# Writing out the four rounds of an attention loop, without the look-ahead of the last one

## The reference, cut to what matters

```python
scores = jnp.einsum('bhqd,bhkd->bhqk', q, k) / jnp.sqrt(jnp.asarray(hd, x.dtype))
causal = jnp.tril(jnp.ones((T, T), bool))
scores = jnp.where(causal, scores, jnp.asarray(-jnp.inf, x.dtype))
attn = jax.nn.softmax(scores, axis=-1)
y = jnp.einsum('bhqk,bhkd->bhqd', attn, v)
```

## Time and profile before

| | |
|---|---|
| median of 3 runs | 2978.18 us (2977.76 to 2980.15) |
| profiled execution, its own time | 2973.09 us |
| its span in the profile | 2971.4 us |
| `attention`, TensorE from the head part's first matmul to the last sum | 839.9 to 2042.0 us |
| the four rounds, on TensorE | 891.2 to 2038.1 us |
| granted TensorE clock, mean over the span | 0.916 |

### The profile page before, as it was taken

One profiled execution on the slowest core, in us unless ns is written; L12 is line 12 of the kernel. 1 busy time (PEld: TensorE's weight loads), 2 busy tenths in 40 slices (PEclk: granted clock), 3 DMA queues, 4 the chain that ended last, 5 costly groups with the idle time before them and its releaser, 6 DMA issues. The chain is left out here.

```text
span 2971.4 us, 45370 instructions
## 1 busy us (share of the span) xinstructions
PE 2544.9 (86%) x13518; PEld 1649.7 (56%) x13519; DVE 1460.8 (49%) x3131; ACT 911.1 (31%) x1734; POOL 1442.0 (49%) x951
## 2 busy tenths in 40 slices
PE   6799999897769999999999999994999239999970
PEld 4677667775534444444444444442777138878860
DVE  4545454012587776777677767774344221111115
ACT  3511001112405555555555556553011010000000
POOL 4443244023236675667566757674233355466413
PEclk9999999998959999999999999997999669999985
DMA  7365655456454241425151515243565474455339
GB/s 259 98 171 169 191 171 185 173 212 205 147 112 102 58 119 42 111 51 126 34 126 39 122 37 126 55 116 114 174 190 166 156 271 163 141 168 171 113 114 394
DMA packets 227095, 422.70 MB, mean 142 GB/s; under 512 B 31596, under 2 KB 82508, under 8 KB 226772
## 3 DMA queue, kind: packets, MB, share of 16 engines
q1 hardware_dynamic: 186116, 283.90, 34.2%
q0 software_dynamic: 25344, 92.29, 8.6%
q10 hardware_dynamic: 15440, 44.09, 3.9%
HBM read 265.72 MB, written 145.53 MB: 138 GB/s over the span
## 5 line engine op out<-in xcount | busy, mean ns | idle before, releaser
L1307 POOL TENSOR_TENSOR t_two<-t_prob 128x1024 f32<-128x1024 f32 (+1 forms) x321 | 686.7, 2161 | 176.1 <-ACT t_prob L1186 111.6
L1186 ACT ACTIVATE t_prob<-t_scores_psum 128x512 f32<-128x512 f32 (+3 forms) x1280 | 618.3, 538 | 471.3 <-PE t_scores_psum L1080 260.2
L1053 PE MATMUL t_seen_psum<-t_k_stack,t_q_stack 97*128 97x512 f32 (+2 forms) x1356 | 561.0, 425 | 49.6 <-DVE t_q_stack L1202 22.6
L1214 DVE TENSOR_REDUCE t_part<-t_seen_psum 128x1 f32<-128x512 f32 x812 | 508.5, 683 | 179.1 <-PE t_seen_psum L1053 170.0
L1076 PE MATMUL t_scores_psum<-t_q_stack,t_k_stack 98*128 98x512 f32 (+3 forms) x1280 | 513.7, 409 | 9.6 <-issue 6.6
L1076 PEld LDWEIGHTS t_scores_psum<-t_q_stack,t_k_stack 98*128 98x128 f32 x1280 | 249.0, 195 | 313.3 <-ACT t_prob L1186 159.9
L1053 PEld LDWEIGHTS t_seen_psum<-t_k_stack,t_q_stack 97*128 97x128 f32 x1356 | 277.9, 205 | 99.2 <-DVE t_part L1214 41.3
L1220 DVE CUSTOM_DVE_ANT_0 t_seen_psum<-t_seen_psum,t_causal 128x128 f32<-128x128 f32 (+3 forms) x544 | 264.4, 505 | 117.1 <-PE t_seen_psum L1053 106.8
L1094 PE MATMUL t_y_acc_psum<-t_prob,t_v 128*32 128x512 f32 (+3 forms) x2576 | 306.2, 548 | 0.0
L670 PE MATMUL e_acc_psum<-e_w_hi,e_x_hi 128*128 128x512 f32 x576 | 231.1, 401 | 0.0
L671 PE MATMUL e_acc_psum<-e_w_lo,e_x_hi 128*128 128x512 f32 x576 | 226.6, 393 | 0.0
(11 more groups left out here) (227 smaller groups left out, 3699.6 us busy)
## 6 DMA issues: line engine op xcount, KB each, us to landing
e_w_raw<-in_expert_w POOLq DMA_DIRECT2D x64, 512.0 KB, 4.4
scratch_rows<-f_y POOLq DMA_DIRECT2D x48, 512.0 KB, 15.1
e_x<-scratch_rows SPq DMA_DIRECT2D x38, 512.0 KB, 4.1
t_q_stack<-scratch_q_hi SPq DMA_DIRECT2D x72, 256.0 KB, 4.8
t_k_stack<-scratch_k_hi SPq DMA_DIRECT2D x72, 256.0 KB, 5.0
scratch_rows<-e_y ACTq DMA_DIRECT2D x36, 512.0 KB, 4.7
f_w_raw<-in_wmod SPq DMA_DIRECT2D x8, 2048.0 KB, 10.8
f_w_raw<-in_w_attn SPq DMA_DIRECT2D x24, 512.0 KB, 7.5
```

Of the source, the lines that this page charges most:

```text
L1053: nc.tensor.matmul(seen[:, n % BANKS, 0:width], q_stack[par][0:SEEN, h, t0:t0 + P], k_stack[par][0:SEEN, h, c * CH:c * CH + width], start= ...
L1186: nc.scalar.activation(prob[:, step % RING, h, c0:CH], scores[:, score_bank(step, h), c0:CH], ACT.Exp, scale=1.0 / math.sqrt(D)).then_inc( ...
L1214: nc.vector.tensor_reduce(dst, seen[:, n % BANKS], AX.X, ALU.max).then_inc(seen_free, 1)
L1307: nc.gpsimd.tensor_tensor(two[:, pair % 2, heads, c0:CH], a, b, ALU.add).then_inc(two_ready, 1)
```

## The change

The four rounds are written out on all five engines: `for i in range(G // 2)` is a Python loop, and i is a number. With that the values that are waited for are constants. A new test, `due(i, n)`, drops the entries of `order` behind the last one of an existing group in the last round: 73 `see` and 2 `turn`, on TensorE, VectorE and SyncE. The loads of steps 40 to 79 of the last round are dropped as well (24 of 256 KB for q and k, 4 of 256 KB for v). The closing waits of SyncE count what is left.

```diff
--- before.py
+++ after.py
@@ -889,7 +889,7 @@
 
         def ended(i, step, lag):
 
-            return [wi for wi in range(-1, 0 if isinstance(i, int) else W) if last_step(wi) == step - lag]
+            return [wi for wi in range(-1, 0 if i == G // 2 else W) if last_step(wi) == step - lag]
 
         def first_column(step):
 
@@ -928,6 +928,11 @@
         HEAD = until(AHEAD)
         entries_of = lambda step: range(until(AHEAD + PACE * step), until(AHEAD + PACE * (step + 1)))
         assert STEPS % RING == 0
+        LAST_OWN = max(n for n, entry in enumerate(order) if entry[1] < 2)
+
+        def due(i, n):
+
+            return i < G // 2 - 1 or n <= LAST_OWN
 
         def share(step, slot):
 
@@ -1016,7 +1021,7 @@
 
                 half, at = divmod(step, STEPS // 2)
                 c, part = divmod(at - Y_LAG, len(PARTS) + 1)
-                if not 0 <= c < NQ:
+                if not 0 <= c < NQ or (half == 1 and i == G // 2 - 1):
                     return
                 par, g = (1, ds(i * 2 + 1)) if half == 0 else (0, ds((i * 2 + 2) % G))
                 if (c, part) == (0, 0):
@@ -1027,21 +1032,21 @@
                     sp.dma_start(v[par][:, c * TPC:(c + 1) * TPC, :],
                                  v_d[g, :, c * TPC:(c + 1) * TPC, :].rearrange("g p k n -> (g p) k n")).then_inc(loaded[par][c], 16)
 
-            with sp.Fori(0, G // 2) as i:
+            for i in range(G // 2):
                 for step in range(STEPS):
                     finish(i, step)
                     fetch(i, step)
                     for n in entries_of(step):
-                        if order[n][0] == "turn":
+                        if order[n][0] == "turn" and due(i, n):
                             sp.wait_ge(minus_ready, i * W + unit_of(order[n]) + 1)
                             load_row(sp, order[n][1] % 2, order[n][2], unit_of(order[n]) % 2)
             for step in range(STORE_LAG + 1):
                 finish(G // 2, step)
             sp.wait_ge(stored, 32 * (G * NQ + 3))
             for c in range(NQ):
-                sp.wait_ge(loaded[0][c], LOADS * (G // 2))
+                sp.wait_ge(loaded[0][c], LOADS * (G // 2 - 1))
             for b in range(2):
-                sp.wait_ge(row_loaded[b], ROW * (G * NQ // 2 + 1 + sum(e[0] == "turn" and unit_of(e) % 2 == b for e in order[:HEAD])))
+                sp.wait_ge(row_loaded[b], ROW * (G * NQ // 2 + 1))
 
         @block.tensor
         def _(pe):
@@ -1086,7 +1091,7 @@
                 wi, kt = steps[step]
                 par, qc = UNITS[wi]
                 c0 = first_column(step)
-                if step >= 0 or isinstance(i, int):
+                if step >= 0 or i > 0:
                     pe.wait_ge(exp_done, (i * STEPS + step) * HG + HG + BANKS)
                 if kt == 0:
                     pe.wait_ge(y_free, i * W + wi + 1)
@@ -1133,11 +1138,13 @@
 
                 for n in share(step, slot):
                     what, dg, qc, c, h, j = order[n]
-                    if what == "see" and dg > 0 and (c, h, j) == (0, 0, 0):
+                    if not due(i, n):
+                        continue
+                    if what == "see" and dg > 0 and (c, h, j) == (0, 0, 0) and (dg < 2 or i < G // 2 - 1):
                         pe.wait_ge(loaded[dg % 2][qc], i * LOADS + LOADS)
                     advance(i, n)
 
-            with pe.Fori(0, G // 2) as i:
+            for i in range(G // 2):
                 for step in range(STEPS):
                     wi = steps[step][0]
                     if steps[step][1] == 0:
@@ -1175,7 +1182,7 @@
                 for wi in ended(i, step, TOTAL_LAG):
                     take_total(i, wi)
 
-            with act.Fori(0, G // 2) as i:
+            for i in range(G // 2):
                 for step in range(STEPS):
                     c0 = first_column(step)
                     act.wait_ge(y_done, i * STEPS + step + 1)
@@ -1269,11 +1276,12 @@
                 for wi in ended(i, step, INV_LAG):
                     invert(i, wi)
 
-            with dve.Fori(0, G // 2) as i:
+            for i in range(G // 2):
                 for step in range(STEPS):
                     for slot in range(HG):
                         for n in share(step, slot):
-                            advance(i, n)
+                            if due(i, n):
+                                advance(i, n)
                         if slot == 1:
                             finish(i, step)
             for step in range(DIVIDE_LAG + 1):
@@ -1320,7 +1328,7 @@
                 for wi in ended(i, step, SPLIT_LAG):
                     split(i, wi)
 
-            with pool.Fori(0, G // 2) as i:
+            for i in range(G // 2):
                 for step in range(STEPS):
                     finish(i, step)
                     if step % 2 == 1:
```

## The result

| | before | after |
|---|---|---|
| median | 2977.97 us (2971.82 to 2980.15, 4 runs) | 2924.17 us (2923.66 to 2929.28, 4 runs) |
| the profiled execution, its own time | 2973.09 us | 2924.26 us |
| its span | 2971.4 us | 2922.4 us |

The ratio is 0.9825, with a 95% interval from 0.9808 to 0.9842. The medians are 53.8 us apart, the two profiled executions 48.8.

A forecast was written before the change was run, and what follows sets the result against it. TensorE was taken to set the pace of the rounds. Turns 30 plus last round 9 made 39 us off the profiled 2973.1, so 2934; with the median 5.1 higher, 2939 us, range 2928 to 2956.

The forecast's parts named there:

- What costs nothing: Register instructions beside busy TensorE, other engines' jumps under its stop, and dropped loads: priced at zero.
- the two terms: The priced gains: 30 us at the three turns between rounds and 9 us in the last round.
- what bounds the kernel: In the rounds of `attention`, TensorE sets the pace, busy 63.34 of the last 63.9 us.
- The turns: Three passages between rounds: 4.2 us of gaps and some 6 of lower clock each, 30 us together.
- the clock falls anyway: Rival at the rounds' first steps: gaps go, clock still drops; gain 22 us, median 2956; 1 in 10.
- the turns stay: Rival at the turns: the stop is not the jump's and remains; 9 us left, 2969; 4 in 100.
- The last round: Last 19 steps of the last round: dropping 73 `see` and two `turn` gives 9 us, lower bound 4.
- The step of 2.62: Last round: a step without row sums takes 2.62 us, where it was 2.85.
- the pair of 6.10: Last round: two steps with 512 columns, without `see`, take 6.10 us, a gain of 0.45 a step.
- Late blocks of code: Rival in the rounds: straight code's 16 KB blocks come late, TensorE stops 2.25 us each; slower; 3 in 100.
- The offset of 5.1 us: Median of the runs before stood 5.1 us above the profiled execution; added to 2934 to give 2939.

The follow-up runs named there:

- tensore_alone_in_the_loop: Against the kernel before: all engines written out except TensorE, which keeps the hardware loop; last round's look-ahead kept. 2972.82 us, ratio 1.0005.
- idle_put_back: Changed kernel, with TensorE made to wait at each turn for two small DMAs one after the other. 2949.59 us, ratio 0.9909 to the kernel before.
- written_out_only: Against the kernel before: rounds written out on all engines, all work and loads of the last round kept. 2931.74 us, ratio 0.9855.
- changed_again: The changed kernel itself, run again on another chip against the kernel before. 2925.68 us, ratio 0.9831.
- idle_put_back_once: Changed kernel, with TensorE made to wait at each turn for one small DMA. 2930.79 us, ratio 0.9845 to the kernel before.
- changed_all_later: Changed kernel with VectorE's addition, GpSimd's split, SyncE's load of a_y and its stores one step later. 2937.63 us, ratio 0.9881 to the kernel before.
- changed_later_addition: Changed kernel with VectorE's addition of a_y and GpSimd's split one step later. 2945.83 us, ratio 0.9893 to the kernel before.

## Why the prediction missed, point by point

- **The step that failed is "What costs nothing"**, the term that was put at zero. In its place the profiles show 8.4 us outside the two terms, and the runs 8 to 10: writing out alone gained 39 and 41, where the turns are 31. The two terms that had a price were right, and so was what bounds the kernel.
- **What bounds the kernel**, TensorE, was right: with all other engines changed and TensorE left in its loop, nothing is gained.
- **The turns**: 30 us forecast, 31.1 in the profiles. The reading by marks held, and so did both halves of it: the jump is needed for the stop (`tensore_alone_in_the_loop`), and a stop without a jump is enough for the lower clock (`idle_put_back`). No "issue" gap is left, and the clock is 1.00 in the first steps, so the rivals "the clock falls anyway" and "the turns stay" are out. The Trainium skill, Advanced Engine Details and Errata, Control Flow Timing, gives about 108 ns for a compare-and-branch, which would have made 0.3 us of the term. The trace does not agree: with the loop on TensorE alone the three taken branches took 3327 to 3777 ns, and their removal brought the whole term. (In the kernel before they took 3303, 3908 and 3421 ns; the 3362 that I gave as the lower end is a median over four, with the branch that isn't taken.)
- **The last round**: 9 us forecast, 9.4 in the profiles and 9.8 against `written_out_only`. The step of 2.62 and the pair of 6.10 were nearly met. Timeline of all engines, one pair of the last round and the wait at its end:

```profile
1962.92 0.96 PE L1081 MATMUL t_scores_psum<-t_q_stack,t_k_stack 98*128 98x512 f32 x3
...
1963.54 2.07 ACT L1193 ACTIVATE t_prob<-t_scores_psum 128x512 f32<-128x512 f32 x4 [1.48 <-PE t_scores_psum L1081]
...
1964.19 0.50 PE L1081 MATMUL t_scores_psum<-t_q_stack,t_k_stack 98*128 98x512 f32 x1 [0.30 <-ACT t_prob L1193]
...
1965.62 0.96 PE L1081 MATMUL t_scores_psum<-t_q_stack,t_k_stack 98*128 98x512 f32 x3
...
1969.15 0.98 PE L1081 MATMUL t_scores_psum<-t_q_stack,t_k_stack 98*128 98x512 f32 x3
...
1990.29 0.64 PE L1112 MATMUL t_total_psum<-t_two,t_ones 128*32 128x256 f32 x8 [1.85 <-POOL t_two L1315]
```

  Head 3's score comes 1.27 us after the first (1.21 forecast) and waits for ScalarE, 0.30 us; a pair takes 1969.15 - 1962.92 = 6.23 us, and its first step 2.70. The last row sums wait 1.85 us for GpSimd, as before. The clock did not fall, though TensorE has more idle time.
- **Late blocks of code** did not come: no "issue" gap stands between the rounds, with q8 at 54 blocks in the 1087 us of the rounds, one in 20 us instead of the 17 forecast. I had overlooked that the written-out code is shorter: q8 brings TensorE's code alone, with 73 blocks in the rounds when TensorE has the loop and 55 when it has not, whatever the others have, and without the loop TensorE's queue has some 3000 instructions fewer there, nearly all on registers.
- **What costs nothing, and did not.** The step priced all the rest at zero, since register instructions lie beside a busy TensorE and other engines' jumps under its stop. The profiles show about 10 us more than the two terms' 39. Of these 1.5 are the terms themselves (31.1 and 9.4 for 30 and 9). About 2 us come from the four middles, and the quietest unit of the kernel, qc 0 of the first round, went from 13.23 to 12.99 us; both have no jump in them (a microsecond or two, I had said, and left it out of the sum). That unit also shows whose instructions count: it takes 13.23 us with TensorE alone written out and 12.98 with TensorE alone in the loop, 13.16 with VectorE alone in the loop, 13.07 with ScalarE and GpSimd, 12.99 with SyncE. So TensorE's own register instructions cost nothing there, as I had said; those of VectorE and of ScalarE and GpSimd, which I had not looked at, cost 0.2 and 0.1 us. The other 7.0 us are in the seven pieces of qc 1 and 2. I had written that `attention` has sevens in the clock's row "besides the turns"; that was misread, for the row has a single 7 there, in the slice in which the rounds end. The low stretches are real, but take a window to be seen, and I opened none between the turns. There is a wait of VectorE for a DMA behind them, which TensorE pays as a gap and, in some places, once more in clock. The changed kernel has less of both in its two profiles, but that this is the missing part was not shown: the wait could not be taken away without a worse one.
- **The offset of 5.1 us** is no step of the mechanism. Adding it comes to the same as taking the 39 off the median of before, 2978 - 39 = 2939. Where that one execution lay was chance: executions of the kernel before range from 2962 to 2985 us over the chips, with medians of 2971.65 to 2977.97, and the changed kernel's profiled execution is 0.1 us off its median in one case and 5.0 us below it in `changed_again`. So of the 15 us between a gain of 53.8 and one of 39, 10 are in the profiles and 5 are spread.

**What stays open.** Where the gain beyond the two terms comes from is not settled. The full changed kernel gained 51 and 54 us, the written-out one 39 and 41 and the dropped look-ahead some 10: these sums agree, so what remains is a part of 8 to 10 us, the 39 to 41 of writing out less the 31 of the turns. It comes with the rounds being written out. It is no sum of parts by engine: TensorE alone written out leaves some 4 us of it, the four others alone nothing, and each of these numbers is uncertain by 4 to 8 us. Leaving one engine or two in the loop did not separate them, the written-out kernel itself varied by 8.7 us between two profiles, and moving the addition replaced the wait by others. That the waits of qc 1 and 2 are behind it was only argued.

## What to carry to other kernels

Price a loop's end on the engine that sets the pace by marks around it, the same steps with and without the jump: the clock behind the stop cost more than the stop. Look for waits like the 1.5 to 1.7 us here elsewhere on that engine, since they can be paid in clock too, and don't call an edit free before you have opened windows on the stretches that it seems not to touch; but follow the queue before you move one, as the DMAs behind the moved wait were late next and cost more. Compare medians with medians and profiles with profiles: where one profiled execution lies beside its median says nothing of the kernel (5.1 us for the one before, 0.1 and 5.0 for the changed one).

## What the runs showed of the hardware that I had not expected

- The price of a stop at a turn does not grow in proportion: 1.25 us of idle time cost 1.3 to 1.4 us, 2.4 us cost 7.2 to 8.7 us, with the clock at 0.50 (1.2 GHz) for 10 to 14 us behind it. Elsewhere the length of a gap does not decide: behind VectorE, gaps of 1.15 and 1.21 us were followed by a low clock in `idle_put_back_once`, and seven of 1.0 to 1.8 us in `changed_all_later` were not. What decides between them was not tried.
- VectorE's addition of two tiles in memory takes 0.69 us alone, and 1.4 to 2.1 us in most units where GpSimd works all the while (`changed_later_addition`, `changed_all_later`).
- The same program, run twice, had 13.7 and 30.7 us of low clock in its rounds.
- TensorE's jump back over 80 steps took 3.3 to 3.9 us in the kernel before and brought two stops, of 2.0 to 2.6 and of 2.1 to 2.3 us, while the jumps of the four other engines, all left in the loop, left the turns within 0.4 us of those without any.
